# A sequence-mixing layer in fp32 on one core: the state product opens the output's bank, VectorE gates from PSUM, and tokens are mixed before the keys' and receptances' products

## The reference, cut to what matters

```python
# block 1: a selective state-space layer, 32 heads of 8, state 64, rank 2
proj = xn @ W_in                       # z, x_raw, B, C, dt, lam, theta
x_raw = silu(x_raw); B, C = rope(rms(B)), rope(rms(C))
y = y_intra(C, B, x_raw) + y_inter(C, S_prev)   # within a chunk; from the state before it
S = cdec * S_prev + st                 # the state is carried from chunk to chunk
y = rms(y * silu(z)); out = y @ W_out

# block 2: a channel mix (keys, receptances, values)
x_prev = x shifted by one token
xr = mu_r * x + (1 - mu_r) * x_prev
xk = mu_k * x + (1 - mu_k) * x_prev
out = sigmoid(xr @ W_r) * (square(relu(xk @ W_k)) @ W_v)
```

## Time and profile before

| what | value |
|---|---|
| median of three runs | 249.6 us |
| the profiled execution | 250.03 us |
| its span, first to last instruction | 248.2 us |
| PE / DVE / ACT / POOL busy | 218.3 / 208.9 / 188.6 / 160.3 us |
| granted TensorE clock, mean | 0.978 of full |

### The profile page before, as it was taken

The page is one execution under the profiler, slowest core; times in us unless marked ns, Lnnn a source line. Parts: engine busy times, 40 slices in busy tenths (PEclk is TensorE's granted clock), DMA queues, the critical chain, the costliest instruction groups (busy, mean ns, idle before and its releaser), DMA issues. The chain is left out here.

```text
span 248.2 us, 6592 instructions
## 1 busy us (share of the span) xinstructions
PE 218.3 (88%) x1962; PEld 159.9 (64%) x1962; DVE 208.9 (84%) x646; ACT 188.6 (76%) x728; POOL 160.3 (65%) x275
## 2 busy tenths in 40 slices
PE   0895998679999999999999999999999999999930
PEld 0893443456767666768777876877687768657920
DVE  1789999987779988986999899989989997956880
ACT  2366776669988699877988798789779977989661
POOL 7433134757798698776769686968686866563530
PEclk9999799999999999999999999999999999999985
DMA  5980000000000000000000001000100110010123
GB/s 121 228 275 4 3 0 0 1 3 1 3 3 3 0 3 1 3 0 5 1 3 0 3 3 45 3 0 1 46 3 1 23 23 0 3 44 4 42 50 87
DMA packets 10199, 6.45 MB, mean 26 GB/s; under 512 B 864, under 2 KB 9856, under 8 KB 10160
## 3 DMA queue, kind: packets, MB, share of 16 engines
q1 hardware_dynamic: 10016, 5.77, 9.6%
q0 software_dynamic: 144, 0.21, 0.4%
HBM read 3.88 MB, written 2.10 MB: 24 GB/s over the span
## 5 line engine op out<-in xcount | busy, mean ns | idle before, releaser
L978 PE MATMUL bank<-x,sg 64*64 64x256 f32 x256 | 35.0, 391 | 0.6 <-DVE sg L1393 0.6
L1386 DVE TENSOR_TENSOR x<-bank,wx 128x512 f32<-128x512 f32 x32 | 21.9, 685 | 15.5 <-ACT bank L672 12.5
L672 ACT ACTIVATE bank<-bank,rsn 128x512 f32<-128x512 f32 x32 | 21.1, 658 | 17.0 <-PE bank L879 17.0
L978 PE MATMUL bank<-xg,sg 64*64 64x256 f32 x256 | 33.0, 376 | 0.0
L966 PE MATMUL pair<-x,turned_bc 64*64 64x256 f32 x224 | 29.6, 376 | 0.0
L544 POOL TENSOR_TENSOR y<-ysum,zs 128x256 f32<-128x256 f32 x32 | 23.8, 742 | 5.5 <-DVE ysum L1409 5.5
L455 POOL TENSOR_TENSOR rb<-mse,halfn 128x2 f32<-128x2 f32 x32 | 23.7, 741 | 2.5
L452 POOL TENSOR_TENSOR mse<-msb,eps_all 128x2 f32<-128x2 f32 x32 | 8.1, 253 | 25.5 <-ACT junk L663 25.4
L1071 PE MATMUL bank<-wo_sb,yt 128*128 128x128 f32 x128 | 22.7, 300 | 0.0
L1386 DVE TENSOR_TENSOR xg<-bank,wx 128x512 f32<-128x512 f32 x32 | 21.8, 680 | 0.0
L427 POOL TENSOR_TENSOR x_lo<-xnT_all,x_hi 128x128 fp32r<-128x128 f32 x32 | 14.7, 460 | 10.4 <-ACT x_hi L587 10.4
(11 more groups left out here) (195 smaller groups left out, 750.2 us busy)
## 6 DMA issues: line engine op xcount, KB each, us to landing
x_all<-x SPq DMA_DIRECT2D x16, 128.0 KB, 4.1
out<-o_all SPq DMA_DIRECT2D x14, 128.0 KB, 2.6
cm<-consts SPq DMA_DIRECT2D x1, 640.0 KB, 6.3
w_sb<-w_in SPq DMA_DIRECT2D x1, 480.0 KB, 4.0
out<-o_all SPq DMA_DIRECT2D x4, 64.0 KB, 2.1
cm<-consts POOLq DMA_DIRECT2D x1, 128.0 KB, 4.0
wo_sb<-w_out SPq DMA_DIRECT2D x1, 128.0 KB, 4.7
bcb_sb<-bc_bias SPq DMA_DIRECT2D x1, 96.0 KB, 4.6
```

Source lines behind the costliest of these rows:

```text
L672: nc.scalar.activation(x_ps[:], x_ps[:], ACT.Silu, scale=rsn[:, par:par + 1]).then_inc(S["x_silu"], 1)
L978: mm = nc.tensor.matmul(y_ps[half(h)], sg[half(h), a, r], rx(x, r)[half(h)], start=start, stop=stop)
L1386: vec.tensor_tensor((x1, xg)[a][:, par].rearrange("p (a e) -> p a e", e=P), x_ps[:].rearrange("p (a e) -> p a e", e=P), wx[:, par, a].unsq ...
```

## The change

The state's share of y no longer has a bank of its own. `state_part(n + 1)` is issued in `mix(n)`, between the two products of `own_token`, and opens the bank of tile n+1's y (banks 6 and 2 alternate); the products within the chunk add to it. The transposes of B and C move to bank 5. ACT's copy `zt`, DVE's sum and POOL's gating go; DVE multiplies y in PSUM by the gate and writes `y`. DVE's four scalings of weights at the start go.

In the second block ACT writes the transposed tokens twice, scaled by 1 - mu_k and by 1 - mu_r, into `shifted`, one column further on. DVE (`mix(u)`) computes `mixed = mu * tokens + shifted` for keys and for receptances, from the transposed tokens in PSUM. PE then has one product for the keys and one per tile for the receptances, with the plain weights. `mix(u)` stands at the end of DVE's step with q = 3, and for units 6, 7 and 8 at three places in `last_ffn`.

```diff
 # POOL
-            def gated(n, q, par):
-                pool.wait_ge(S["ysum_ready"], n + 1)
 ...
-                nc.gpsimd.tensor_tensor(y[:, par], ysum[:, par], zs[:, q], ALU.mult).then_inc(S["y_ready"], 1)
 # ACT
-            def state_part(n, par):
 ...
-                nc.scalar.activation(zt[:, par], inter_ps, ACT.Copy).then_inc(S["zt_sb"], 1)
 ...
-                nc.scalar.activation(curT[:, b], x_t, ACT.Copy).then_inc(C["tr_sb"], 1)
-                nc.scalar.activation(prevT[:, b, 1:], x_t[:, :, 0:L - 1], ACT.Copy).then_inc(C["shifted"], 1)
+                for m in range(2):
+                    nc.scalar.activation(shifted[:, within_chunk_of(m, u), 1:], turned_ps(u), ACT.Identity,
+                                         scale=one_less_mu[:, 1 - m:2 - m]).then_inc(C["tr_sb"], 1)
 # PE
+            def state_part(n):
 ...
+                pe.wait_ge(S["t_sb"], n + 1)
+                wait_past(pe, S["y_ready"], n - 1)
+                from_state(n % 2, st[:, n % NQ], False).then_inc(S["inter_ps"], 1)
 ...
                 earlier_tokens(0)
-                state_product()
+                next_state(0)
                 earlier_tokens(1)
-                pe.wait_ge(S["p_added"], min(n, NT - NQ))
-                next_state(0)
+                next_state(1)
                 pe.wait_ge(S["xg_ready"], n + 1)
                 own_token(0)
-                next_state(1)
+                if n + 1 < NT:
+                    state_part(n + 1)
                 own_token(1).then_inc(S["y_ps"], 1)
 ...
-                    nc.tensor.matmul(k_ps, w_cur[:, 0], cur[:, columns(u)], start=True, stop=False)
-                    nc.tensor.matmul(k_ps, w_prev[:, 0], prev[:, columns(u)], start=False, stop=True)\
+                pe.wait_ge(C["mixed"], 2 * u + (2 if u < 6 else 1))
+                nc.tensor.matmul(ffn_bank("k", u)[:, 0:n_of(u) * 128], wk_sb[:], mixed_k[:, columns(u)], start=True,
 ...
-                    nc.tensor.matmul(r_ps, cur[:, at_i], w_cur[:, 1], start=True, stop=False)
-                    mm = nc.tensor.matmul(r_ps, prev[:, at_i], w_prev[:, 1], start=False, stop=True)
+                    mm = nc.tensor.matmul(r_ps, mixed_r[:, at_i], wr_sb[:], start=True, stop=True)
 # DVE
-            def summed_y(n, par, general):
+            def gated_y(n, q, par, general):
 ...
+                vec.tensor_tensor(y[:, par], yk[:] if general else y_ps[par], zs[:, q], ALU.mult).then_inc(S["y_ready"], 1)
 ...
+            def mix(u):
+
+                dve.wait_ge(C["tr_sb"], 2 * u + 2)
+                for m, used in enumerate(("k_ps", "r_ps")):
+                    wait_past(dve, C[used], ahead(u) + 1)
+                    vec.scalar_tensor_tensor(out=mixed[m][:, sequences(u)], in0=turned_ps(u), scalar=mu_sb[:, 1 - m:2 - m],
+                                             in1=shifted[:, within_chunk_of(m, u), 0:L], op0=ALU.mult,
+                                             op1=ALU.add).then_inc(C["mixed"], 1)
```

## The result

The changed kernel takes 259.25 us (median of 4 runs, 259.16 to 261.18), the kernel before 249.57 in the same job: 1.0388 times as long, 95% interval 1.0354 to 1.0423. The forecast was 250.5, the range ended at 253.5. Slower was the likeliest of the three outcomes; the size is far off.

A forecast was written before the change was run, and what follows sets the result against it. PE's queue was taken to bound the loop, with DVE nearly full. Terms -2.4 + 1.1 - 0.1 - 0.9 + 3.2 = +0.9 us on 249.6 gave 250.5 us; range 246.8 to 253.5.

The forecast's parts named there:

- The state product, "I take 0": TensorE's state product per tile only moves in the queue, between the same kind of neighbours: 0 us.
- A chunk: Loop of four-tile chunks: PE's saved 1.75 us eaten by mixing and PE's stand; 23.45 us against 23.5, -0.1 over four.
- relief: Loop: POOL without y disturbs DVE's L1457 less, about 0.35 us off a chunk's 23.8.
- A: Rival, loop: POOL's disturbance of L1457 goes, chunks of 22.7 us, 247.4 us in all; chance 0.18.
- C: Rival, DVE's mixing: disturbed by POOL, 0.27 us more each, about +3.4 us, 253.9 in all; chance 0.14.
- Before the first mixing, -2.4: Start: POOL's y no longer delays PE, and ACT's square comes earlier; 2.4 us won, bounds 1 and 4.
- First mixing, +1.1: Step where mixing comes in: keys wait for DVE's mixings behind its rotations, a pure loss of 1.1 us.
- Last chunk, -0.9: Last chunk: no tile follows, DVE has room, so the receptances' saved 0.9 us count in full.
- The end, +3.2: End: late statistics and mixings against PE's saved products, +3.2 us; bounds +1 and +5.
- The first term: End: unit 6's statistics start 2.7 us late, behind unit 5's mixing.
- the three terms (2.8 + 0.8 - 3.1): End: 2.8 us mixings of units 6 to 8, 0.8 waiting for ACT's copies, less 3.1 of PE's saved products.
- B: Rival, end: PE is the bound and late statistics are caught up; end costs 1.0, 248.3 us in all; chance 0.14.

The follow-up runs named there:

- product alone: Only the state product and gating half of the change, on the kernel before; keys and receptances as before: 246.12 us, ratio 0.9868.
- mixing alone: Only the mixing half (shifted copies on ScalarE, mixing on VectorE, one product each), on the kernel before: 258.76 us, ratio 1.0351.
- filled_gaps: The whole change plus unused products in TensorE's gaps before the keys' products of units 0 to 4 and the last transposes of y: 253.56 us, ratio 1.0183.
- keys_later: The whole change with the keys' product of units 0 to 4 moved behind the next step's x projection: 251.14 us, ratio 1.0048.
- product half with tile 0's mask first: Product alone with tile 0's mask ahead of the token weights' scalings and, in step 1, transposes behind the projection: 245.07 us, ratio 0.9814.

## Why the prediction was wrong, step by step

The forecast for the span was +0.9 us, measured +9.3. Of the 8.4 us between them the clock behind the stands is 5.5, the start 3.7, the end at full clock 0.8 and the first mixing at full clock 0.4; the chunks at full clock (1.1), the last chunk (0.3) and the time up to tile 0 (0.6) go the other way.

- *TensorE's clock: missing from the sum.* I worked with the durations at 2.4 GHz throughout. That TensorE would stand about 2 us before each keys' product was forecast and came (2.13 to 2.23); that it can run at 1.2 GHz behind it was not. Filling the gaps returned 5.5 us in these places. This is the largest error. In the start the clock fell as well, which is part of the term on the start below.
- *The state product, "I take 0".* The step failed, though in the direction that makes the kernel faster. I said that the product "needs tile n+1's turned B and C, which the old one waited for too", and did not price that wait, because PE's busy time shows none: I read that PE issues without a pause. In the old place the wait lengthens the block by 0.2 to 0.4 us per tile; in the new one the copy has long ended. That is 1.1 us per chunk in product alone, 4.4 in all. The Trainium skill (TensorEngine Tiling (Array Packing), section Key Properties) says that different tiles of the array can load weights and multiply in parallel. The trace agrees: a state product that is ready starts 0.02 us behind the token product (69.20 and 69.22), and one that has to wait leaves it without a partner (150.11 and 150.58). In the whole change 1.5 us of the 4.4 are lost even at full clock, where a chunk's length runs through VectorE's mixing.
- *A chunk: right in its mechanism, mis-sized in one term.* My 23.8 us per chunk without relief is what mixing alone shows: 23.87. The relief was 0.35 in my sum and 0.7 in fact: 23.18 in the change with gaps filled. L1457 became shorter as I said (mean 0.53 us instead of 0.60 from 112 to 182 us, 0.3 us per chunk); the rest I put down to the shorter block, which no run separates. DVE's wait for silu went down to one of 0.92 us per chunk in filled_gaps, as the sign says, but is 2.39 to 2.54 us where the clock fell. Signs A (under 22.9 us) and C (mixing over 0.9 us) did not appear; mixing took 0.74 us, 0.66 from start to start, against my 0.675. It takes 0.74 to 0.75 us in every unit of 512 columns, while L1457 there still ranges from 0.34 to 0.72.
- *Before the first mixing, -2.4: wrong.* POOL's waits went. But the change also made the transposes of B and C wait for the mask, since their bank is the scores' now, and the mask stands behind VectorE's preparations in the first steps. I had not costed this wait. It is 4.8 us in four times, and the start came out at +1.3. Part of this is the clock, at 0.50 from 48 to 50 us: keys_later, the same up to tile 12 but with the clock at 1.00 there, has 60.44 instead of 61.15. In the product half with tile 0's mask first the start was -0.3, still 2.1 us above my sum, and what holds it there stays open.
- *First mixing, +1.1.* At full clock it is +1.5 (7.75 against 6.29), mixing alone +1.6; the other 1.35 us are the clock's. Where the further 0.4 us come from stays open.
- *Last chunk, -0.9.* Right: mixing alone shows -0.9. The change has -1.2, and product alone -0.4, which I had at 0.
- *The end, +3.2.* At full clock +4.0, with the clock +4.8. The first term was right: transposes of unit 6 late by 2.4 us (2.7 forecast for the statistics). The last term failed: I gave TensorE's 3.1 us of saved products back, but TensorE is not the bound there; even at full clock (filled_gaps) it waits 1.29, 1.01 and 0.54 us for VectorE's mixings. From the transposes of unit 6 to the last residuals of unit 5 it took 11.84 us, and 11.00 in filled_gaps, instead of 9.0; I had +0.5 for the three terms (2.8 + 0.8 - 3.1). That the end's total at full clock is only 0.8 us off is partly luck: this stretch is 1.5 us longer than I had it, the transposes 0.3 less late, and behind the residuals 0.4 us were saved that I had not counted. The sign for B (residuals no more than 15.5 us behind the last mask) stayed away: they came 20.2 us behind its end.

## What to carry to other kernels

A new wait on TensorE has two prices: the stand, and what TensorE does behind it if the clock falls. Read the granted clock behind each stand, and if real work can be put into the gap, put it there (here: keys behind the next projection, 259.3 to 251.1 us). Take a change with two halves apart before judging it: here one half wins 1.3%, the other loses 3.5%, and together they lose more than their sum. A busy engine can hide a wait: compare a block's length, from first start to next start, in places where its operands come early and late. Where a tensor moves to another bank, cost every wait that the new neighbour brings, in the first steps as well as in the steady state.

## What the runs showed of the hardware

- After TensorE had stood for 2.13 to 2.23 us the granted clock fell to 1.2 GHz three times out of five; after 1.80 to 2.17 us in mixing alone, never in five. At a stand of 1.46 us in the start it fell in the change and not in keys_later, which has the same program up to there. The length of the stand alone does not decide it here; what does stays open.
- At 1.2 GHz a product of 128x512 of the projection took 0.63 us instead of 0.39, the first behind the keys 1.41 instead of 0.80.
- Products of 64x64 quadrants that are queued alternately start 0.01 to 0.02 us apart when both are ready. A tile's 28 passes of token and state products and 8 of scores take 1.99 us then; where the second in the queue has to wait for its operand, up to 2.43 in the loop.

The fastest version that was run is the product half with tile 0's mask first, 245.07 us, 1.9% under the kernel before; product alone, 246.12, is the same within the measurement.
